# Four small VectorE instructions read their constants from a tile instead of carrying them as immediates

## The reference

```python
h = token_mixer(x)                        # 8 x 344 x 64
h = h + retention(layer_norm(h))
h = h + product_key_attention(layer_norm(h))
# the last one, for each of 8 heads and 8 batches:
#   similarities of each token with 2 x 64 keys; the best 16 of either half; of their 256 sums the best 16
#   softmax over these 16; k, v = weighted sums of the table rows that the sums point to (4096 rows a head)
#   causal attention over the 344 tokens, output projection
```

## Time and profile before

| what | value |
| --- | --- |
| median of 3 runs | 2059.56 us (2059.18 to 2062.91) |
| the profiled execution's own time | 2059.58 us |
| its span, first to last instruction | 2057.8 us |
| PE busy | 1942.7 us (94%) |
| DVE busy | 1724.5 us (84%) |
| ACT busy | 1486.5 us (72%) |
| POOL busy | 1265.2 us (61%) |
| granted TensorE clock, mean | 0.974 |

### The profile page before, as it was taken

One profiled execution on the slowest core, in us unless ns is written; L12 is line 12 of the kernel. 1 busy time (PEld: TensorE's weight loads), 2 busy tenths in 40 slices (PEclk: granted clock), 3 DMA queues, 4 the chain that ended last, 5 costly groups with the idle time before them and its releaser, 6 DMA issues.

```text
span 2057.8 us, 43660 instructions
## 1 busy us (share of the span) xinstructions
PE 1942.7 (94%) x11396; PEld 1509.4 (73%) x11396; DVE 1724.5 (84%) x5163; ACT 1486.5 (72%) x3091; POOL 1265.2 (61%) x1300
## 2 busy tenths in 40 slices
PE   5996649999999999999999999999999999999997
PEld 3983437777777777777777777777777777777776
DVE  3562659999989989999999899999999899999996
ACT  3564236787777777777777777787778777777775
POOL 2440106667766666677677667666766666676664
PEclk9998768999999999999999999999999999999998
DMA  3000030000100020001000100001000100010001
GB/s 97 1 0 0 1 103 16 18 14 19 62 20 19 19 62 18 18 17 59 18 19 19 58 23 19 19 19 60 17 17 16 60 19 19 19 61 19 19 17 27
DMA packets 118154, 58.06 MB, mean 28 GB/s; under 512 B 109712, under 2 KB 116048, under 8 KB 116813
## 3 DMA queue, kind: packets, MB, share of 16 engines
q1 hardware_dynamic: 115298, 56.75, 10.2%
q10 hardware_dynamic: 2795, 0.70, 0.2%
HBM read 24.55 MB, written 0.70 MB: 12 GB/s over the span
## 4 chain that ended last, share of the span: by engine, by line
PE 79%; issue 2%; DVE 1%; SPq 1%; DMA 1%; POOL 1%; ACT 1%; DVEq 0%; ACTq 0%; POOLq 0%
PE ps L988 27%; PE ps L996 15%; PE ps L979 15%; PE ps L1000 7%; PE ps L1038 4%; PE ps L1056 3%; PE ps L973 2%; PE ps L1048 2%; PE ps L1023 2%; SPq L931 1%; DMA k_X<-k_spl 1%; PE ps L1010 1%; PE ps L1016 1%; POOL k_W_low L1322 0%; PE ps L1039 0%
## 5 line engine op out<-in xcount | busy, mean ns | idle before, releaser
L1322 POOL TENSOR_TENSOR k_W_low<-k_W,k_W_high 128x688 fp32r<-128x688 f32 x513 | 852.3, 1661 | 379.0 <-ACT k_W_high L1164 379.0
L1159 ACT ACTIVATE k_W<-ps 128x688 f32<-128x688 f32 x1029 | 765.6, 744 | 391.3 <-PE ps L979 373.9
L1441 DVE SCALAR_TENSOR_TENSOR k_W<-ps,k_W 128x688 f32<-128x688 f32 x1028 | 888.8, 865 | 164.0 <-ACT k_W L1159 144.4
L988 PE MATMUL ps<-k_W,k_tab 128*128 128x344 f32 x2048 | 676.9, 453 | 0.0
L979 PE MATMUL ps<-k_X,k_sel 128*128 128x344 f16 x2058 | 473.8, 312 | 26.7 <-DMA k_X<-k_spl 13.5
L988 PEld LDWEIGHTS ps<-k_W,k_tab 128*128 128x128 f32 x2048 | 367.2, 190 | 127.2 <-issue 0.6
L1164 ACT ACTIVATE k_W_high<-k_W 128x688 fp32r<-128x688 f32 x513 | 395.4, 771 | 0.0
L996 PE MATMUL ps<-k_W_high,k_tab_high 128*128 128x344 f32 x1024 | 385.7, 379 | 0.0
L979 PEld LDWEIGHTS ps<-k_X,k_sel 128*128 128x128 f16 x2058 | 170.9, 99 | 216.0 <-issue 82.6
L996 PE MATMUL ps<-k_W_high,k_tab_low 128*128 128x344 f32 x1024 | 324.9, 320 | 0.0
L1000 PE MATMUL ps<-k_W_low,k_tab_high 128*128 128x344 f32 x1024 | 244.4, 320 | 0.0
(11 more groups left out here) (228 smaller groups left out, 2567.3 us busy)
## 6 DMA issues: line engine op xcount, KB each, us to landing
k_tab<-in_tables SPq DMA_DIRECT2D x9, 2048.0 KB, 7.2
k_X<-k_spl SPq DMA_TRANSPOSE x390, 2.4
k_xs<-x2T SPq DMA_DIRECT2D x33, 172.0 KB, 2.1
k_qT<-k_qs SPq DMA_DIRECT2D x33, 86.0 KB, 2.0
cst<-in_consts SPq DMA_DIRECT2D x1, 1024.0 KB, 19.0
wts<-in_weights SPq DMA_DIRECT2D x1, 896.0 KB, 13.0
cst<-in_consts SPq DMA_DIRECT2D x1, 874.5 KB, 16.7
xr<-in_xrows SPq DMA_DIRECT2D x1, 750.0 KB
```

The source lines that it names most:

```text
L988: mm = mm_(sums, tab[:, slot, at + k, :], W[:, d % RING, k, :], start=(d == 0 and k == 0), stop=(d == NDC - 1 and k == 1))
L1159: A(W[:, d % RING, :, :], ps[:, 2 * (d % 2):2 * (d % 2) + 2, 0:LOUT], ACT.Exp).then_inc(e_done, 1)
L1322: G.tensor_tensor(W_low[:, q % SPLIT_RING, :, :], W[:, d % RING, :, :], W_high[:, q % SPLIT_RING, :, :].bitcast(F32), ALU.subtract).then_i ...
L1441: V.scalar_tensor_tensor(W[:, d % RING, :, :], ps[:, 2 * (d % 2):2 * (d % 2) + 2, 0:LOUT], 0.0, W[:, d % RING, :, :], ALU.is_ge, ALU.mult) ...
```

## The change

Four instructions of VectorE took their scalar constants as immediates. Now a tile `bounds` of four columns holds them, filled once by four memsets in VectorE's prologue, and the instructions name its columns: two columns in each of the two clamps, one in each of the two `floors`. The shapes, the order of all instructions and every wait in the loop stay; the two waits for `zeroed` in VectorE's prologue count four more.

```diff
         off = sb("off", [128, NT])
+        bounds = sb("bounds", [128, 4])
+        UPPER, LOWER, MARGIN, DEPTH = (bounds[:, k:k + 1] for k in range(4))
...
                 def floors(n):
-                    V.tensor_scalar(small[:, AM, :], small[:, AM, :], -DELTA, None, ALU.mult).then_inc(top_step, 1)
-                    V.tensor_scalar(small[:, FLOOR, :], fin[:, :, 0], -80.0, None, ALU.add).then_inc(top_step, 1)
+                    V.tensor_scalar(small[:, AM, :], small[:, AM, :], MARGIN, None, ALU.mult).then_inc(top_step, 1)
+                    V.tensor_scalar(small[:, FLOOR, :], fin[:, :, 0], DEPTH, None, ALU.add).then_inc(top_step, 1)
...
                 def clamp_scores(n):
                     dve.wait_ge(a_ready, n * 2 + 2)
-                    V.tensor_scalar(aS[:, :, 4, :], aS[:, :, 0, :], -NEG, FAR, ALU.min, ALU.max).then_inc(clamped, 1)
+                    V.tensor_scalar(aS[:, :, 4, :], aS[:, :, 0, :], UPPER, LOWER, ALU.min, ALU.max).then_inc(clamped, 1)
                     dve.wait_ge(clamped, n * 2 + 1)
-                    V.tensor_scalar(aS[:, :, 0:4, :], aS[:, :, 0:4, :], -NEG, FAR, ALU.min, ALU.max).then_inc(clamped, 1)
+                    V.tensor_scalar(aS[:, :, 0:4, :], aS[:, :, 0:4, :], UPPER, LOWER, ALU.min, ALU.max).then_inc(clamped, 1)
...
                 V.memset(zz[:, :], 1.0).then_inc(zeroed, 1)
+                for bound, value in ((UPPER, -NEG), (LOWER, FAR), (MARGIN, -DELTA), (DEPTH, -80.0)):
+                    V.memset(bound, value).then_inc(zeroed, 1)
...
-                dve.wait_ge(zeroed, 10)
+                dve.wait_ge(zeroed, 14)
```

## The result

The changed kernel takes 2084.71 us (median of 4 runs, 2084.19 to 2085.71), the kernel before 2059.98 us (median of its 4 runs, the new one beside it included). The ratio of the runs is 1.011, with a 95% interval of 1.0083 to 1.0137: slower by 1.1%, 24.7 us. The forecast was 2085.7 us. Runs of one kernel scatter by up to 20 us, three far slower executions aside, and most of that comes from before the loop: the loop's first `floors` starts 317 to 322 us after the beginning in nine of the thirteen profiles and 332 to 334 us after it in the other four, where the granted TensorE clock from 100 to 314 us was 0.77 or 0.78 (0.81 in the profiles of the kernel before and the changed one); from 400 to 1900 us it was 1.00 in each profile.

A forecast was written before the change was run, and what follows sets the result against it. TensorE was taken to bound the kernel, waiting at step 3 of each item for weights behind `floors`. 64 x 0.40 = 25.6 us plus 0.5 for the prologue, on 2059.6, gave 2085.7 us, range 2060 to 2089.

The forecast's parts named there:

- TensorE bounds the loop, and step 3 has no slack against `floors`: TensorE, step 2 to 3: waits 0.17 us for VectorE's weights, so each 0.1 us more in `floors` lengthens the item 0.1.
- The pointer form still uses the port: `floors` and clamps: changed instructions still wait for what GpSimd holds, as L1501 did in the prologue (518 ns, usually 261).
- rival 3: `floors` and clamps: pointer operands take the instructions off the port, 10.9 us less in the loop, 2049.2 us; chance 0.10.
- The pointer is read before the port is asked for, so a long wait hides it: L1415 and L1428: waits of 0.72 and 1.17 us hide the pointer read, and both keep their ends.
- Rival 2: L1416: pointer read hidden behind the instruction before, so it asks for the port as early as now; 2060.1 us, chance 0.07.
- One pointer costs 0.06 us, two 0.10: Price on a VectorE instruction that doesn't wait: 0.06 us for one pointer (`floors`), 0.10 for two (clamps).
- L1416 loses to L1275 and ends 0.02 us behind it: Second `floors` instruction asks too late, waits for GpSimd's L1275 and ends at 1019.85, not 1019.45: 0.40 us an item.
- rivals 1 and 4: L1416 keeps the port, 2063.9 us, chance 0.14; or loses to both L1275 and L1294, about 2128.6 us, chance 0.03.
- The step that carried the risk: GpSimd's instruction takes the port at age 0.115 to 0.14 us; L1416 by pointer asks at 0.17, a margin of 0.03.
- The clamps are covered, by 0.26 us: Clamps L1428 and L1430: TensorE needs the weights behind them 0.26 us later, so 0.10 us more (at most 0.21) costs nothing.
- Sum: Whole kernel: 64 x 0.40 = 25.6 us for the loop plus 0.5 for the prologue, 26.1 us more, 2085.7 us.
- Start order: L1416 against L1275: by first start L1416 (1019.30 against 1019.32) would keep the port; the forecast held that starts don't decide.

The follow-up runs named there:

- the last experiment: Each `floors` instruction written as three of one element, in the kernel before (immediates, 2051.14 us) and in the changed kernel (pointers, 2056.79 us).
- four of the experiments: Kernel before with first `floors` instruction widened to 3 x 12 (2063.19 us) or 3 x 18 (2063.06), a memset between (ratio 1.0009), or second clamp done twice (2079.76).
- the kernel with 3 x 18 elements: Kernel before, all immediates, with the first `floors` instruction widened to 3 x 18 elements of its own tile; one run, 2063.06 us.
- 3 x 24 elements: Kernel before, all immediates, with the first `floors` instruction widened to 3 x 24 elements of its own tile; one run, 2081.85 us.

## Why the prediction was right

- *TensorE bounds the loop, and step 3 has no slack against `floors`*: right. TensorE's way there grew from 1.33 to 1.75 us (the medians of the loop too), VectorE's from L1416's start to the weights' from 0.07 to 0.46, and the item by 0.39.
- *The pointer form still uses the port*: right. L1417 and L1430 wait as their immediate forms did (884 and 1395 ns, before 879 and 1391), and L1418 could not have waited otherwise. So rival 3 is out.
- *The pointer is read before the port is asked for, so a long wait hides it*: right. The kernel with five of six pointers and none on the depth shows no loss, and its L1417 still takes 0.88 us. Rival 2, a read hidden behind the instruction before, is out: single elements with pointers start 0.12 us apart, with immediates 0.06.
- *One pointer costs 0.06 us, two 0.10*: 0.06 (159 to 218 ns; 0.12 in place of 0.06 from start to start in the last experiment) and 0.12 (226 to 343, 426 to 545). The second term was a little small, under its cover.
- *L1416 loses to L1275 and ends 0.02 us behind it*: right in all 64 items (550 to 556 ns), which puts rivals 1 and 4 out. The step that carried the risk, GpSimd's age when it takes the port, was a little low: I read at most 0.14 us from rounded rows of one instance in the prologue, which is 0.146 at the trace's full resolution, and the runs put it at 0.144 to 0.151. The changed kernel's 0.17 to 0.18 is beyond either, so it didn't matter. But the margin was some 0.02 us, and it was partly luck that so thin a one held: the first item of the loop in four of the experiments shows that the age isn't all that decides.
- *The clamps are covered, by 0.26 us*: measured 0.27.
- *Sum*: 64 x 0.40 + 0.5 was forecast and 24.7 us measured, 25.1 against the 2059.6 us that the forecast started from. By the profiles it is 64 x 0.39 = 24.9 for the loop, and in the prologue the way from the last old memset (L1493, now L1495) to the first log weights grew by 0.33 us (21.47 to 21.80), where I took 0.5. Both terms were a little high.
- *Start order*: the page "SBUF — State Buffer" of the Trainium skill, section "Who interferes with whom", has whoever issues first keep the shared pair. By the starts in the trace (when each was issued it doesn't show) that fails both ways. L1418 starts at 1031.58, before L1277 at 1031.60, and waits for it. In the kernel with 3 x 18 elements, VectorE and then GpSimd:

```profile
1156.32 0.16 DVE L1417 TENSOR_SCALAR k_small<-k_fin 128x3 f32<-128x3 f32 x1
```
```profile
1156.31 0.53 POOL L1276 TENSOR_TENSOR k_aS<-k_sS,k_top 128x192 f32<-128x192 f32 x1
```

VectorE's starts after GpSimd's and doesn't wait. What the page says of an exclusive hold for the whole instruction the traces bear out; VectorE's ends 0.022 to 0.027 us behind GpSimd's in all 64 items of the changed kernel. Only the order doesn't go by the starts. It fits a moment inside each instruction, by an estimate from the durations 0.13 us after the start for VectorE's immediate form, 0.19 with a pointer and some 0.15 for GpSimd's, with the first items of the loop as the exception.

## What to carry to other kernels

Look for short VectorE instructions with long durations: where their minimum is far under their median and their end follows a GpSimd instruction's by a few hundredths of a microsecond, they are waiting for GpSimd, and neither the idle time nor the list of waits tells it. Before such an instruction in front of a bound engine is made even slightly longer, see what GpSimd starts in that gap, because the price of losing it is what is left of GpSimd's next instruction, here 0.40 us for 0.06; and see whether the work can be put in one-element pieces, which did not wait here. Two pointers on an instruction that waited anyway, or that had cover, cost nothing here.

## What the runs showed of the hardware

- A per-partition constant by pointer costs a VectorE `tensor_scalar` 0.06 us (at 1 and at 3 elements), two cost 0.12 (at 96 and at 384), and nothing in an instruction that waits for GpSimd for longer than that.
- `tensor_scalar` instructions of 3, 96 and 100 elements in SBUF waited while a GpSimd `tensor_tensor` ran (879, 1391 and 518 ns against 159, 226 and 261); one-element ones didn't, in 195 instances each of four lines (at most 149 ns with an immediate and 211 with a pointer). A one-element instruction with an immediate follows the one before by 0.06 us.
- With both engines after the port, who gets it turned over within 0.01 us of VectorE's start (behind GpSimd's `weights_low`, 3 x 18 against 3 x 24 elements), and in one kernel fell both ways from item to item. Where VectorE got it late, GpSimd's instruction grew from 510 to as much as 547 ns.
- A one-element memset behind a waiting instruction took next to no time: the next instruction started some 0.01 us later than it does without it.
- The second clamp's copy into a scratch tile took 553 ns, where the clamp takes 426 (416 in the same run) for the same 384 elements from the same source; its destination lies in one piece, the clamp's own in three. I hadn't expected a cost there and did not follow it up.
